# A two-layer graph network on one Trainium2 core: edge ranges counted in half precision, ranked from one table, with row factors computed on GpSimd

## The reference

```python
def reference(x, src, dst, edge_type_2, ...):       # x: 625 x 512 float32; 10000 edges, sorted by dst
    edge_index = jnp.stack([src, dst])
    xn = _layernorm(x, axis=-1)                      # (x - mean) / sqrt(var + 1e-5)
    x = x + rgcn_two_layers(xn, edge_index, edge_type_2, ...) + mixer(xn[None], ...)[0]
    ...

def rgcn_gate_layer(x, row, col, edge_type, basis, att, gate_w, root, bias):
    w = jnp.einsum('rb,bio->rio', att, basis)        # 30 bases of 512 x 512, 2 relations
    x_j = x[col]                                     # row = src, col = dst
    for r in range(2):
        gate = jax.nn.sigmoid(x_j @ gate_w[r, :, 0])
        msgs.append(gate[:, None] * x_j @ w[r])
    msg = jnp.where((edge_type == 0)[:, None], msgs[0], msgs[1])
    return jax.ops.segment_sum(msg, row, num_segments=625) + x @ root + bias
```

## Time and profile before

| | us |
|---|---|
| median of 3 runs | 846.35 |
| the three runs | 844.45, 846.35, 1033.0 |
| profiled execution, its time | 843.48 |
| profiled execution, span of its instructions | 841.7 |
| mean granted clock of TensorE in it | 0.974 of full |
| TensorE busy (matmul) | 800.7 |
| VectorE busy | 539.5 |
| ScalarE busy | 248.6 |
| GpSimd busy | 148.2 |

### The profile page before, as it was taken

One profiled execution on the slowest core, in us unless ns is written; L12 is line 12 of the kernel. 1 busy time (PEld: TensorE's weight loads), 2 busy tenths in 40 slices (PEclk: granted clock), 3 DMA queues, 4 the chain that ended last, 5 costly groups with the idle time before them and its releaser, 6 DMA issues.

```text
span 841.7 us, 10823 instructions
## 1 busy us (share of the span) xinstructions
PE 800.7 (95%) x3995; PEld 640.9 (76%) x3995; DVE 539.5 (64%) x743; ACT 248.6 (30%) x468; POOL 148.2 (18%) x96
## 2 busy tenths in 40 slices
PE   4999999999999999999998999997699999999997
PEld 3988766847477777765767778897598888888886
DVE  5876998979989999999777426068541111511112
ACT  4252223316411013222045332142432321432310
POOL 2011001120100000002201350031343330433300
PEclk9999999999999998999999999999589999999999
DMA  7533779796878768742041120000242120322001
GB/s 245 213 50 47 227 214 337 266 276 158 240 228 276 246 220 282 242 139 100 1 159 58 48 97 1 1 2 1 100 151 96 55 98 2 100 100 100 0 0 61
DMA packets 64211, 110.21 MB, mean 131 GB/s; under 512 B 6815, under 2 KB 16412, under 8 KB 64172
## 3 DMA queue, kind: packets, MB, share of 16 engines
q1 hardware_dynamic: 54476, 96.71, 34.5%
q0 software_dynamic: 6912, 7.70, 5.4%
q10 hardware_dynamic: 2784, 5.27, 1.7%
HBM read 105.81 MB, written 1.28 MB: 127 GB/s over the span
## 4 chain that ended last, share of the span: by engine, by line
PE 89%; DVE 6%; issue 2%; ACT 1%; POOL 1%; DVEq 0%; POOLq 0%
PE bank L1310 55%; PE bank L1730 13%; PE bank L1396 6%; PE bank L1511 4%; PE bank L1528 3%; PE bank L1522 2%; PE bank L1505 2%; PE bank L1326 1%; DVE st L890 1%; PE bank L1437 1%; PE bank L1333 1%; DVE slot L987 1%; ACT slot L581 1%; DVE slot L885 0%; DVE slot L1116 0%
## 5 line engine op out<-in xcount | busy, mean ns | idle before, releaser
L1004 DVE SCALAR_TENSOR_TENSOR weights<-weights,att 128x2048 f32<-128x2048 f32 x116 | 268.9, 2392 | 2.7 <-DMA weights<-in_L_gnn_basis 2.1
L1291 DVE CAST hid_hi<-slot 128x626 fp32r<-128x626 f32 x32 | 15.6, 487 | 160.7 <-ACT slot L846 160.7
L1310 PE MATMUL bank<-half,ew_hi 128*128 128x314 f32 (+1 forms) x512 | 114.0, 312 | 2.2 <-POOL ew_lo L550 2.2
L1310 PE MATMUL bank<-AT,slot 125*128 125x312 f32 (+1 forms) x400 | 105.9, 426 | 0.8 <-ACT slot L711 0.8
L1310 PEld LDWEIGHTS bank<-AT,slot 125*128 125x128 f32 x400 | 75.5, 189 | 31.0 <-ACT slot L711 1.0
L550 POOL TENSOR_TENSOR ew_lo<-weights,ew_hi 128x1024 fp32r<-128x1024 f32 x28 | 69.4, 2500 | 134.4 <-ACT ew_hi L828 134.4
L1310 PEld LDWEIGHTS bank<-half,ew_hi 128*128 128x128 f32 x512 | 88.4, 193 | 5.6 <-issue 2.9
L581 ACT ACTIVATE slot<-bank 128x312 f32<-128x312 f32 (+6 forms) x88 | 43.8, 525 | 148.7 <-PE bank L1310 128.9
L1310 PE MATMUL bank<-weights,slot 128*125 128x512 f32 (+5 forms) x306 | 86.9, 447 | 0.3 <-ACT slot L581 0.3
L846 ACT ACTIVATE slot<-bank,eb_now 128x312 f32<-128x312 f32 x64 | 33.3, 522 | 157.2 <-PE bank L1310 157.2
L1310 PE MATMUL bank<-half,ew_lo 128*128 128x312 f32 (+1 forms) x256 | 79.5, 310 | 0.0
(11 more groups left out here) (297 smaller groups left out, 1116.4 us busy)
## 6 DMA issues: line engine op xcount, KB each, us to landing
weights<-in_L_gnn_basis SPq DMA_DIRECT2D x60, 1024.0 KB, 5.5
weights<-in_L_ffn_W SPq DMA_DIRECT2D x32, 512.0 KB, 4.5
weights<-in_L_mix_kqv_w SPq DMA_DIRECT2D x1, 3072.0 KB, 10.2
weights<-in_w_qkvT SPq DMA_DIRECT2D x3, 1024.0 KB, 5.4
slot<-slot POOLq DMA_DIRECT2D x10, 250.0 KB, 6.5
weights<-in_L_mix_mlp_w ACTq DMA_DIRECT2D x2, 1024.0 KB, 13.6
weights<-in_L_gnn_root ACTq DMA_DIRECT2D x2, 1024.0 KB, 8.7
slot<-in_row_mlp_b POOLq DMA_DIRECT2D x1, 1250.0 KB, 26.1
```

The lines of the kernel that those rows point to most:

```text
L1004: ins = dve.scalar_tensor_tensor(wrel[layer][r], wmat(at), att[:, layer, r, b:b + 1], wrel[layer][r], ALU.mult, ALU.add)
L1310: ins = pe.matmul(out, a, b, start=i == 0, stop=i == len(pairs) - 1)
```

## The change

Seven edits, all at the beginning of the kernel. (1) `pres` and `gez` are float16, and the count is a float16 matmul with `ones16`. (2) GpSimd makes `ones16`, a table of ranks `rank2` (1..20 upwards and 20..1 downwards, for each tile) and `zero` ahead of its other constants, and signals `first_consts`; TensorE waits for that alone before the count, and for `consts` only before the transposes after block 1. (3) The ranges come from one maximum over both rank tables in place of a maximum and a minimum one after the other. (4) The five `keyf` rows, and the wait for `consts`, stand behind the ranges. (5) TensorE opens block 0's banks ahead of its wait for `ranges`; in every block the register load stands behind the opening matmuls. (6) `row_factors()` leaves VectorE; GpSimd does the same work with `pow(sd, -1)` and products, as soon as `x_std` comes. (7) The second square root takes its 1/H as a scale.

```diff
+        minus1 = sb("minus1", [P, TT])
...
-        pres = tmp[0:P, 0, 0:TT * ET].rearrange("p (j t) -> p j t", j=TT)
-        gez = tmp[0:P, 1, 0:TT * ET].rearrange("p (j t) -> p j t", j=TT)
+        pres, gez = (tmp[0:P, i, 0:TT * ET // 2].bitcast(f16).rearrange("p (j t) -> p j t", j=TT) for i in range(2))
+        rank2, held2 = (tmp[0:1, i, 256:256 + 2 * TT * EG].rearrange("p (i j q) -> p i j q", i=2, j=TT) for i in range(2))
...
+            pool.memset(ones16[:, :], 1.0)
+            pool.iota(rank2[:, 0, :, :], pattern=[[0, TT], [1, EG]], base=1, ...)
+            pool.iota(rank2[:, 1, :, :], pattern=[[0, TT], [-1, EG]], base=EG, ...)
+            pool.memset(zero[:, :], 0.0).then_inc(S("first_consts"), 1)
             link(pool.memset(ident[:, :], 0.0))
             link(pool.memset(ones[:, :], 1.0))
-            link(pool.memset(zero[:, :], 0.0))
+            pool.memset(minus1[:, :], -1.0)
...
-            link(pool.memset(ones16[:, :], 1.0))
...
+            pool.wait_ge(S("x_std"), 1)
+            link(pool.tensor_tensor(rs[0:P, :], sd[0:P, :], minus1[:, :], ALU.pow))
+            pool.tensor_tensor(nmr, x_mean, rs[0:P, :], ALU.mult)
+            link(pool.tensor_tensor(hv, x_sum, rs[0:P, :], ALU.mult))
+            pool.tensor_tensor(hv, hv, rs[0:P, :], ALU.mult).then_inc(S("h_var"), 1)
+            pool.wait_ge(S("h_std"), 1)
+            pool.tensor_tensor(hv, sd[0:P, :], minus1[:, :], ALU.pow).then_inc(S("h_rs"), 1)
             pool.wait_ge(S("xn_row"), 5)
...
-            act.activation(sd[0:P, :], hv, ACT.Sqrt, bias=eps[0:P, 1:2]).then_inc(S("h_std"), 1)
+            act.activation(sd[0:P, :], hv, ACT.Sqrt, bias=eps[0:P, 1:2], scale=1.0 / H).then_inc(S("h_std"), 1)
...
-            link(dve.tensor_copy(srcf, edges[:, 0, :]))
+            dve.tensor_copy(srcf, edges[:, 0, :])
...
-            for j in range(TT):
-                ins = dve.tensor_scalar(keyf[:, j, :], relf, -float(P * j), None, ALU.add)
-            link(ins)
-            dve.wait_ge(S("consts"), 1)
...
-            link(dve.tensor_scalar(rr, rr, 0.5, None, ALU.is_ge))
-            link(dve.scalar_tensor_tensor(t40, iq, 1.0, rr, ALU.add, ALU.mult))
-            link(dve.tensor_reduce(last, t40, AX.X, ALU.max))
-            link(dve.scalar_tensor_tensor(t40, iq, -float(EG), rr, ALU.add, ALU.mult))
-            link(dve.tensor_reduce(first, t40, AX.X, ALU.min))
-            link(dve.tensor_scalar(first, first, float(EG), float(EG - 1), ALU.add, ALU.min))
-            link(dve.tensor_tensor(last, last, first, ALU.subtract))
-            link(dve.tensor_scalar(last, last, 1.0, None, ALU.max))
+            for i in range(2):
+                ins = dve.scalar_tensor_tensor(held2[:, i, :, :], rr, 0.5, rank2[:, i, :, :], ALU.is_ge, ALU.mult)
+            link(ins)
+            link(dve.tensor_reduce(most.rearrange("p (i j) -> p i j", i=2), held2, AX.X, ALU.max))
+            link(dve.tensor_scalar(back, back, 1.0, -1.0, ALU.max, ALU.mult))
+            dve.tensor_scalar(first_of, back, float(EG), None, ALU.add)
+            link(dve.scalar_tensor_tensor(groups_of, last, -float(EG), back, ALU.add, ALU.subtract))
+            link(dve.tensor_scalar(groups_of, groups_of, 1.0, None, ALU.max))
             dve.tensor_copy(rng_i[0:1, 0:10], rt2).then_inc(S("ranges"), 1)
+            for j in range(TT):
+                ins = dve.tensor_scalar(keyf[:, j, :], relf, -float(P * j), None, ALU.add)
+            link(ins)
             dve.wait_ge(S("ranges"), 1)
+            dve.wait_ge(S("consts"), 1)
...
-                if j == 0:
-                    row_factors()
...
-            pe.wait_ge(S("consts"), 1)
+            pe.wait_ge(S("first_consts"), 1)
             bk = claim(pe, "rng")
             pe.wait_ge(S("presence"), 1)
-            group(bk[0:1, 0:TT * ET], [(ones[0:P, 0:1], pres.rearrange("p j t -> p (j t)"))]).then_inc(S("psum_full"), 1)
-            pe.wait_ge(S("ranges"), 1)
-            for j in range(TT):
-                groups = pe.value_load(rng_i[0:1, j:j + 1], min_val=1, max_val=EG)
+            group(bk[0:1, 0:TT * ET], [(ones16[0:P, 0:1], pres.rearrange("p j t -> p (j t)"))]).then_inc(S("psum_full"), 1)
+            for j in range(TT):
                 stage, n = A_BLOCK[j]
                 ...                                             (the opening matmuls, as before)
+                if j == 0:
+                    pe.wait_ge(S("ranges"), 1)
+                groups = pe.value_load(rng_i[0:1, j:j + 1], min_val=1, max_val=EG)
                 with pe.Fori(0, groups) as i:
...
                 if j == 1:
+                    pe.wait_ge(S("consts"), 1)
                     to_cols("hT", row(3), "h_row")
```

17 lines of the change are left out of this document (5 added, 12 removed).

## The result

The changed kernel takes 841.61 us (median of 20 runs), the kernel before 845.14 us beside it on the same chip (20 runs): a ratio of 0.9967 with a 95% interval of 0.9953 to 0.9982. The predicted time was 843.0 and the predicted gain 2.4 us; the medians differ by 3.5 us, and the ratio makes 2.8 us, from 1.5 to 4.0 by its interval. The profiled execution of the changed kernel took 838.86 us, span 837.1, against 843.48 and 841.7: 4.6 us less, at the same mean clock of 0.974 (by their clock records each spends 46 us in sum at the lower level of TensorE's clock).

The account below looks back on a forecast made before the run. TensorE was taken as the bound from the first kq product on, so only time saved before block 4 closes at 84.1 us counts. Terms 1.9 + 0.4 + 0.4 + 0 - 0.3 = 2.4 us gave 843.0 us from 845.4, range 839.5 to 848.

Parts of the forecast that it names:

- first one-hot matmul: Head, up to block 0's first one-hot matmul: from 13.89 to 12.0, a gain of 1.9 us, 1.4 to 2.6.
- slow stretch: TensorE's slow matmuls in block 0, 15.4 to 19.6: moves with the start, same length; 0.95 lost to 1.8 us gained.
- block 0 to block 1: TensorE's 0.80 us wait for block 1's one-hots: gain 0.4 us, from a loss of 1.75 to a gain of 0.80.
- first bias DMA: GpSimd's issue moves to about 24.8 in block 0, costing TensorE 0.9 instead of 1.32: gain 0.4 us, 0 to 1.3.
- second bias DMA: Issued at about 51 to 56, start of block 2, with the same 1.35 us cost: gain 0, bounds -0.7 to +1.35.
- loads of blocks 2 and 3: TensorE's register loads, now behind the openings: loss 0.3 us in block 2 (0 to 1.7), 0 to 0.65 in block 3.
- VectorE adds up from about 6.5, not from 5.6: of the half precision, only 0.1 us shows: Head, reduction over the count: VectorE's preparations end at 6.52, after the count; this joint gains 2.1 us, possibly 2.5.
- The factors on GpSimd: Five GpSimd operations after `x_std`, 1.1 us up to `h_var`: buy nothing by themselves, price on VectorE taken as zero.
- Everything falls into traffic: Rival: early bias DMAs slow register loads of blocks 1 to 4; 2.5 us slower, 847.9 us; chance 0.2.
- ends at its old time: Rival: block 0's slow stretch still ends at 19.6, so the gain is 1.4 us, 844.0 us; chance 0.2.
- More goes away: Rival: slow stretch ends sooner, block 1 gains 0.8, a bias DMA is hidden; gain 6 us, 839.4 us; chance 0.15.
- the count would wait as before: Rival, head: half precision hidden, keys take back the ranges' saving, count still waits; 0.4 + 0.4 left, 844.6 us; chance 0.05.

Follow-up runs that it names:

- again: The changed kernel once more, nothing altered, for a second trace: 839.62 us, ratio 0.9939 to the kernel before.
- count_f32: The changed kernel with the count and its two tables in float32 again, ones made first: 839.84 us, ratio 0.9949 to the kernel before.
- early_only: The kernel before with one edit: ones and zero are GpSimd's first constants and TensorE's count waits for them only: 841.76 us, ratio 0.9975.
- load_first: The changed kernel with the register loads of blocks 1 to 4 ahead of the opening matmuls again: 840.54 us, ratio 0.9936 to the kernel before.
- count_f32_keys_first: count_f32 with the five key rows ahead of VectorE's reduction again: 838.35 us, ratio 0.9943 to the kernel before.
- first_placed_busy_wait: first_placed plus 20 matmuls of zeros behind block 0's openings, in TensorE's wait for the ranges: 839.32 us, ratio 0.9923 to the kernel before.
- first_placed: The changed kernel with the first bias DMA held until block 1 is closed and register loads ahead of the openings: 841.51 us, ratio 0.9931.
- factors_dve: The changed kernel with the factors back on VectorE behind block 0's one-hots: 841.17 us, ratio 0.9961 to the kernel before.
- bias_placed: The changed kernel, first bias DMA held until block 1 is closed, second until block 4 is, register loads ahead of the openings: 840.31 us, ratio 0.9953.
- bias_late: The changed kernel with both bias DMAs issued only once block 4 is closed: 867.48 us, ratio 1.0252 to the kernel before.

## Why the prediction was right, by its own steps

| term of the sum, us | forecast | first trace | again |
|---|---|---|---|
| first one-hot matmul | +1.9 (1.4 to 2.6) | +3.04 | +2.51 |
| slow stretch | 0 (-0.95 to +1.8) | +0.60 | +0.57 |
| block 0 to block 1 | +0.4 (-1.75 to +0.8) | -0.25 | +0.43 |
| first bias DMA | +0.4 (0 to +1.3) | +0.39 | +0.35 |
| second bias DMA | 0 (-0.7 to +1.35) | +0.27 | -0.09 |
| loads of blocks 2 and 3 | -0.3 (-2.35 to 0) | +0.02 | -0.26 |
| ahead of block 4 | none | +0.42 | +0.43 |
| dip of the clock in block 1 | none | -1.67 | 0 |
| sum at kq | +2.4 | +2.82 | +3.94 |

The measured columns are differences between starts in the traces: of the first matmul of each block and of its closing, less the hold-ups where a block has two terms. The slow stretch's 0.60, for one, is what is left of the head's gain at block 0's closing: 38.14 - 35.86 = 2.28 = 3.04 - 1.36 + 0.60. How block 0 is split between this row and the first bias DMA is an estimate: if the hold-up there costs as much beyond TensorE's idle time as it did in block 1 before, 0.4 us go from the DMA's row to the stretch's. And the stretch's length differs by 3.3 us between kernels with the same instructions there, so its gain can't be put down to an edit.

**The term that was mis-sized is the first one.** The mechanism held: the count at once behind `presence`, the reduction behind VectorE's preparations, the rank products, the keys, the loads. "VectorE adds up from about 6.5, not from 5.6: of the half precision, only 0.1 us shows" is the step that failed. The preparations' end, 6.52, was read off a trace in which two of them, lines 935 and 937, were unusually long (0.37 and 0.71). In the two traces of the changed kernel the preparations end at 5.38 and 5.95, the short count at 5.28 and 5.57; a long one would end 1.0 us later, behind both. So the count's length does show, and count_f32 measures it at 0.78 us. The prediction saw that the 0.71 might shrink to 0.25, but took that for its upper bound and not for its value. It even named the reason, that GpSimd's constants fall otherwise: both long rows end 0.05 us behind a GpSimd instruction that had begun before them or with them (5.24 against 5.19, 6.24 against 6.19). So the step took two waits for GpSimd for fixed lengths. Neither the early count (0.71 again in early_only) nor the types (0.48 in count_f32) shorten the multiply; where GpSimd's instructions fall does. The ranges were well sized (2.30 forecast; 2.28 from 5.42 to 7.70), the keys 0.75 forecast and 0.62 measured. Ranges to first one-hot without the keys took 1.89, forecast 1.49 + 0.25.

**Block 0 to block 1** went as the prediction's bounds had it, and not as its value, in the first trace: DMA traffic had come over the quiet place, and one load took over 1.2 us. In the second trace the gain was the forecast 0.4. Traffic alone does not make a load long: in count_f32, under the same DMA, VectorE's two took 0.32 and 0.31. The Trainium skill (DMA: Bandwidth & Descriptors, Latency and other measured facts) gives these loads a floor of about 600 ns; of the changed kernel's five at line 977 the median is 319 ns and the longest 1386, so the traces disagree with it; the longest loads all stand in DMA traffic.

```profile
L977 DVEq TENSOR_LOAD <-rng_i x5: 301/319/1386, 9.2 to 71.8; - x5
```

**The factors on GpSimd** bought nothing, as said. Up to `h_var` they took 2.3 us where 1.1 were forecast, because a `pow` on 125 x 5 takes 1.33 us there and a product 0.21 to 0.42; ScalarE waited 2.43 for them, all of it hidden. The bias DMA went out at 25.84 for 24.8 by the same difference. "I take zero" for VectorE's price was right: its one-hots kept 0.38 and 0.28 us through all five operations. The Trainium skill (SBUF — State Buffer, "SBUF: two separate sides") says that GpSimd and VectorE, in certain modes, exclude each other for a whole instruction, from which the prediction estimated up to 1 us there; the trace shows none for these small operations beside the float16 one-hots. It shows a hold-up beside the 3.36 us issue of the DMA, with 1.3 us for each of three VectorE instructions, and one at the head, where the multiply by 625 took 0.48 or 0.71 and not 0.20.

**The first bias DMA** was said to cost 0.9 in block 0, because VectorE leads by four buffers. It cost 1.36 (1.40 again): three VectorE instructions were hit, and the lead covered less than was thought. But its old place had cost more than 1.32, too: block 1 took 10.44 us before and 8.69 without hold-up and dip, which is 1.75. The two errors cancel, and that the gain is the forecast one is luck. **The second** was to cost its 1.35 in another place. Its hold-up there is 1.10 and 1.45, and block 2 is longer by 1.30 and 1.66; block 3, its old place, is shorter by 1.57.

**The load behind the openings** costs 0.4 us in block 2 and 0.3 in block 3 against load_first, forecast 0.3 and about nothing; against the kernel before, block 2 loses nothing, since the load that took 2.12 us there took 0.31 here. **Ahead of block 4** TensorE had 0.36 us of idle time before, which is gone: VectorE's loads took 1.00 and 0.54 us there before, and 0.31 and 0.30 now. The prediction said only that VectorE is later there anyway, and gave it no term.

**The rivals.** "Everything falls into traffic" had its mechanism in part, loads of 1.23 and 1.39 us, but its average of 1.6 us a load was not reached: the medians of the changed kernel's loads are 428, 319 and 485 ns. The stretch that "ends at its old time" is refuted: it ended at about 15 and not at 19.6. "More goes away" came nearest in its parts (0.6 from the stretch, 0.6 to 1.1 more at the start); its sum has 0.6 and 1.5 where its words say only 1.8 for the stretch. That the count would wait as before is refuted by its row. And what no case had is the clock: the dip in block 1 took 1.67 us back, one at 170 us gave 1.7. The sum was 0.4 us short in a trace with the dip, 1.5 in one without it, so that the first trace comes so near to 2.4 is luck. Over all runs the gain was 3.5 us by the medians and 2.8 by the ratio and by span times clock, 0.4 to 1.1 more than forecast: both traces of the changed kernel, 4.6 and 4.0 us ahead of the kernel before at the end, lie on its fast side.

**No clearly better version came out of it.** The lowest medians are 838.35 (count_f32_keys_first), 839.32 (first_placed_busy_wait) and 839.62 (the changed kernel again), and their intervals overlap one another.

## What to carry to other kernels

Where two paths meet, each length read off a trace is the length under that trace's neighbours: price the shorter path by its nearest short rows as well, before you call it hidden. A step that is moved to another queue takes along what is queued behind it, here two 1.25 MB additions, and these cost TensorE 1.1 to 1.5 us beside one-hots and far more behind them, where the DMAs issued after them land up to 38 us late. A long row next to another engine's row that ends with it is a wait, not work. And where a kernel's own clock dips weigh 1.7 us each, a gain of 1 us is read from the marks of two traces of each kernel, or from span times clock, not from a median.

## What the runs showed of the hardware

- The granted clock falls to the lower of its two levels (0.50 of 2.4 GHz) for 3.4 us or longer (6.8 us from 164.5 in load_first, 10.2 from 422.2 in first_placed, 27.3 from 589.6 in the kernel before). Every trace has a dip that begins at 187 to 195 us; others come in one execution and not in the next: at 38 to 42 us in the first trace of the changed kernel, behind 1.05 us of idle time, and not in the second, behind 0.36. Idle time alone doesn't decide it: behind 0.80 us at the same place there is a dip in factors_dve and none in both traces of the kernel before. At 170 us both traces of the kernel before have one, at 166 several others, count_f32 none from 162 to 178. One of 3.4 us costs 1.7. The spans of the kernel before go with the runs' mean clock: 838.9 to 841.3 us in the 22 runs with 0.974 or more, 842.0 to 845.6 in the 36 with less.
- The slow stretch at the start of block 0 is the same lower level (468 ns a matmul, as in the dips; 296 later), but the clock record begins only where it ends, and the views print 1.00 ahead of that.
- VectorE's float32 multiply of 125 x 80 takes 0.20 us at its shortest, and 0.48 or 0.71 when a GpSimd memset or iota has begun first: it ends 0.05 us behind it. Float16 one-hots kept their 0.38 and 0.28 us beside GpSimd's small products and `pow`.
- A register load from `rng_i` takes 0.30 us when the DMA engines are quiet. In traffic it takes 0.3 us to 2.3 (before) and 2.7 us (factors_dve).
- GpSimd's `pow` on 125 x 5 elements costs 1.22 to 1.33 us, three to six times a product (0.21 to 0.42).
- A GpSimd-issued DMA of 1250 KB that adds takes 25 to 27 us to land in the head, and 32 to 40 us beside the 1 MB basis loads. The median of those loads is 5.3 to 5.5 us in all kernels but bias_placed, where it is 6.2; the longest single one is 14.5 us in the kernel before and 33.4 in bias_late.
